# Four-layer graph network in one kernel: the third layer's rows in edge order, two PSUM banks per copy in every merge, and projected and normalised row as one 2 KB line per node

## What is computed

```python
h = jnp.maximum(_layernorm(x, axis=-1), 0.0)          # every layer begins so
...
proj_s = feature @ W_s.T                               # third layer, feature = h
proj_t = feature @ W_t.T
z = proj_s[src] + proj_t[dst]
z = jnp.where(z >= 0, z, NEG_SLOPE * z)
e = (z @ W_attn.T)[:, 0]
...                                                    # softmax of e over the edges of one source: alpha
msg = feature[src] * alpha[:, None]
agg = jax.ops.segment_sum(msg, dst, num_segments=n)
return agg @ W_fc.T + b_fc
```

## Time and profile before

| | us |
|---|---|
| median of 3 runs (lowest, highest) | 7961.38 (7960.68, 7969.36) |
| the profiled execution: its time | 7962.39 |
| the profiled execution: its span, first instruction to last | 7960.7 |
| node pass of the third layer | 847 |
| score pass | 1034 |
| merge 0 / 1 / 2 / 3 | 540 / 595 / 601 / 502 |

### The profile page before, as it was taken

The page is one execution under the profiler, slowest core; times in us unless marked ns, Lnnn a source line. Parts: engine busy times, 40 slices in busy tenths (PEclk is TensorE's granted clock), DMA queues, the critical chain, the costliest instruction groups (busy, mean ns, idle before and its releaser), DMA issues. The chain is left out here.

```text
span 7960.7 us, 152645 instructions
## 1 busy us (share of the span) xinstructions
PE 5847.9 (73%) x22090; PEld 3555.4 (45%) x22091; DVE 5333.9 (67%) x17864; ACT 3368.9 (42%) x10659; POOL 4364.3 (55%) x5571
## 2 busy tenths in 40 slices
PE   4997899847779997777999777777657679400477
PEld 3773244335534443554444344444225558400365
DVE  5999888745579994456666566666954569533755
ACT  1993255315645552454444333333113567300166
POOL 1556777700022224766777677776567653577443
PEclk8996699979999998999999989888888999755799
DMA  2664333459867775787989766665026877522177
GB/s 61 211 209 134 101 102 105 133 169 312 298 212 249 251 248 195 261 298 260 314 310 314 267 202 202 204 205 178 2 68 227 291 256 227 138 55 54 56 228 235
DMA packets 897753, 1560.81 MB, mean 196 GB/s; under 512 B 129481, under 2 KB 638654, under 8 KB 897575
## 3 DMA queue, kind: packets, MB, share of 16 engines
q1 hardware_dynamic: 572230, 858.57, 32.8%
q10 hardware_dynamic: 188000, 410.91, 14.9%
q0 software_dynamic: 137344, 289.63, 12.9%
HBM read 861.24 MB, written 697.48 MB: 196 GB/s over the span
## 5 line engine op out<-in xcount | busy, mean ns | idle before, releaser
L1431 PE MATMUL merge_banks<-merge_rows,merge_mask 128*128 x6264 | 1573.5, 406 | 631.9 <-SPq L1362 301.6
L1431 PEld LDWEIGHTS merge_banks<-merge_rows,merge_mask 128*128 128x128 f32 x6264 | 1220.3, 201 | 985.0 <-issue 814.0
L2133 PE MATMUL node_p_out<-w,node_h_t 128*128 128x259 f32 (+2 forms) x4704 | 1434.5, 427 | 9.3 <-ACT node_h_t L2172 7.9
L1413 DVE TENSOR_SCALAR merge_mask<-ramp,dst_at,soft_at_step 128x128 f32<-128x128 f32 x2349 | 839.2, 363 | 874.6 <-PE merge_banks L1431 735.6
L1495 ACT COPY merge_total<-merge_banks 128x256 f32<-128x256 f32 x1568 | 577.4, 369 | 1024.3 <-PE merge_banks L1431 866.6
L1575 POOL DMA_INDIRECT merge_rows<-h,merge_take_i x816 | 784.9, 962 | 317.9 <-issue 210.2
L2046 POOL TENSOR_TENSOR node_inv_std<-node_var,node_minus_half 128x4 f32<-128x4 f32 x392 | 433.5, 1106 | 886.0 <-DVE node_var L1981 567.9
L2133 PEld LDWEIGHTS node_p_out<-w,node_h_t 128*128 128x128 f32 x4704 | 744.4, 190 | 261.7 <-issue 207.0
L2111 PE MATMUL node_p_turn<-ident,node_xn 128*128 128x128 f32 x3136 | 620.7, 280 | 196.5 <-DVE node_xn L1938 96.1
L2133 PE MATMUL node_p_out<-w,node_kept_t 128*128 128x512 f32 x1568 | 741.7, 596 | 0.0
L2111 PEld LDWEIGHTS node_p_turn<-ident,node_xn 128*128 128x128 f32 x3136 | 403.2, 141 | 748.9 <-issue 463.0
(11 more groups left out here) (563 smaller groups left out, 11087.8 us busy)
## 6 DMA issues: line engine op xcount, KB each, us to landing
merge_held<-own ACTq DMA_DIRECT2D x196, 512.0 KB, 5.8
x<-merge_total ACTq DMA_DIRECT2D x196, 512.0 KB
node_x<-x SPq DMA_DIRECT2D x196, 512.0 KB, 6.0
node_x<-in_x SPq DMA_DIRECT2D x194, 512.0 KB
merge_rows<-h_by_edge SPq DMA_DIRECT2D x408, 128.0 KB
h<-node_rows_h SPq DMA_DIRECT2D x98, 516.0 KB, 4.2
h_by_edge<-rank_src_of_src SPq DMA_DIRECT2D x49, 1024.0 KB
merge_held<-h ACTq DMA_DIRECT2D x98, 512.0 KB, 5.7
```

What stands on the lines that cost most here:

```text
L1413: ins = nc.vector.tensor_scalar(mask[j][:], k.ramp[:, 0:P], columns(k.dst_at, s), columns(weight, s), ALU.is_equal, ALU.mult)
L1431: nc.tensor.matmul(banks[:, bass.ds(nc.s_assert_within(at[2 * j + 1], 0, (BANKS - 1) * 512, skip_runtime_bounds_check_because=small), D)], ...
L2133: ins = nc.tensor.matmul(p_out[w][g % banks][:, 0:n], turned_rows(q.h, g)[:, c * P:(c + 1) * P], matrix[:, c, :], start=c == 0, stop=c == 1)
```

## The change

It has four parts.

1. In every merge ACT copies two banks per instruction, for the flush as for the seed (`two_banks`): it waits for the last step of the second tile of the pair. `flush_at` keeps every second entry, so that a read of it brings 8 entries.
2. In every merge the first two groups of base rows are loaded and the banks seeded from them, and only then the other twelve loads are issued.
3. The third node pass writes the normalised row next to the projected one, in `out`, and stores both as one line of 2 KB per node (`pair2`). `kept_t` and its store are gone; the cut rows lie in four buffers `h_t` as in the other layers.
4. The score pass gathers those 2 KB lines. PE turns the normalised half of each gathered tile (two transposes), ACT cuts it at zero, PE multiplies by the third matrix, and the product is stored as `by_edge`, one row for each edge. So merge 2 loads its rows in order by SP, as merge 0 does, and POOL keeps only the release loop there. POOL's gathers wait for the turn as well as for the sum.

The core of the diff:

```diff
@@ merge
-                nc.scalar.copy(bank(q, g), held[q.held][:, g, :]).then_inc(seeded, 1)
+                nc.scalar.copy(two_banks(q, g), held[q.held][:, g:g + 2, :]).then_inc(seeded, 2)
...
-                    at[:] = counts(act, flush_at, H * G, min(4, TURN - q.w) * G)
+                    at[:] = counts(act, flush_at, H * (G // 2), min(4, TURN - q.w) * (G // 2))
...
-                for g in range(G):
-                    act.wait_ge(steps, at[q.w % 4 * G + g])
+                for g in range(0, G, 2):
+                    act.wait_ge(steps, at[(q.w % 4 * G + g) // 2])
...
-                    nc.scalar.copy(total[q.total][:, g, :], bank(q, g)).then_inc(kept, 1)
+                    nc.scalar.copy(total[q.total][:, g:g + 2, :], two_banks(q, g)).then_inc(kept, 2)
...
-            for n in range(HELD):
+            for n in range(2):
                 hold(At(0, n))
             act.wait_ge(opened, BANKS)
             for n in range(2):
-                for g in range(G):
+                for g in range(0, G, 2):
                     seed(At(0, n), g)
+            for n in range(2, HELD):
+                hold(At(0, n))
@@ node_pass
-    out = both("out", {0: [P, 1, G, D + 3], 1: [P, 1, G, D], 2: [P, 2, G, D], 3: [P, 1, G, P + 8]}[layer])
+    out = both("out", {0: [P, 1, G, D + 3], 1: [P, 1, G, D], 2: [P, G, 3, D], 3: [P, 1, G, P + 8]}[layer])
...
-                    parts = [out[q.h][:, n] for n in range(2)] + [biased[q.h][:]]
+                    parts = [out[q.h][:, :, 0:2, :].rearrange("p g n f -> p g (n f)"), out[q.h][:, :, 2, :], biased[q.h][:]]
...
-                if layer == 2:
-                    sp.dma_start(turned_group(tables[3], q.H), kept_t[q.h][:].rearrange("p g f -> p (g f)")
-                                 ).then_inc(t_put[q.h], 16)
@@ score_sources
-    a, b = ([ph.sb(f"{n}{j}", [P, D]) for j in range(R)] for n in "ab")
+    a, b = ([ph.sb(f"{n}{j}", [P, w]) for j in range(R)] for n, w in (("a", 2 * D), ("b", D)))
...
                         pool.wait_ge(added, t + LAG - R)
+                        pool.sem_inc(turn_pool, 1)
+                        pool.wait_ge(turned, t + LAG - R)
                         pool.sem_inc(turn_pool, 1)
...
+                    if j % LAG == 0:
+                        pe.wait_ge(got[j // LAG], 16 * 2 * LAG * (i + 1))
+                    turn(t, j, first)
                     if not (first and j < 2):
+                        multiply(t - 2, (j - 2) % R, first and j >= 2)
+                    if not (first and j < 3):
+                        place(t - 3, (j - 3) % R, first and j >= 3)
...
                         lower(t - 1, (j - 1) % R, first)
+                        rectify(t - 1, (j - 1) % R, first and j >= 1)
@@ gnn_kernel
-        merge(nc, k, "merge2", own2, x3, table=h2, weight=at_step)
+        merge(nc, k, "merge2", own2, x3, ordered=by_edge, weight=at_step)
```

More of the change, by code:

```diff
@@ L1472, in hold, with two_banks @@
                     act.dma_start(held[q.held][:], tile_rows(base, q.group() * ROWS)).then_inc(held_got[q.held], 16)
-            def bank(q, g):
+            def two_banks(q, g):
                 first = q.side * G + g
-                return banks[:, first * 512:first * 512 + D]
+                return banks[:, first * 512:(first + 2) * 512].rearrange("p (n f) -> p n f", n=2)[:, :, 0:D]
             def seed(q, g):
@@ L1770, in node_pass, with normal @@
     minus_half = ph.sb("minus_half", [P, G])
-    if layer == 2:
[L1772 to L1778, removed]
-    out = both("out", {0: [P, 1, G, D + 3], 1: [P, 1, G, D], 2: [P, 2, G, D], 3: [P, 1, G, P + 8]}[layer])
+    h_t = [ph.sb(f"h_t{n}", [P, D]) for n in range(G)]
+    out = both("out", {0: [P, 1, G, D + 3], 1: [P, 1, G, D], 2: [P, G, 3, D], 3: [P, 1, G, P + 8]}[layer])
     junk = [ph.sb(f"junk{n}", [P, D]) for n in range(2)]
+    def normal(side, g):
+        return out[side][:, g, 1, :] if layer == 2 else xn[side][:, g, :]
     p_turn = [ph.ps(f"p_turn{n}", [P, 512]) for n in range(2)]
@@ L2166, in rectify @@
                 act.wait_ge(turned, t + 1)
-                if layer == 2:
-                    if not q.new and g == 0:
-                        act.wait_ge(t_put[q.h], 16 * n_put * q.i)
-                elif not q.first:
+                if not q.first:
                     act.wait_ge(product, t - G + 1)
-                nc.scalar.activation(turned_rows(q.h, g), p_turn[g % 2][:, 0:D], ACT.Relu).then_inc(rectified, 1)
+                nc.scalar.activation(h_t[g][:], p_turn[g % 2][:, 0:D], ACT.Relu).then_inc(rectified, 1)
             def work(q):
@@ L2187, in work @@
                     if layer == 2:
-                        nc.scalar.copy(out[q.h][:, 0:2, g, :], p_out[0][g % banks][:].rearrange("p (n f) -> p n f", n=2)
+                        nc.scalar.copy(out[q.h][:, g, 0::2, :], p_out[0][g % banks][:].rearrange("p (n f) -> p n f", n=2)
                                        ).then_inc(out_made, 1)
@@ L2357, in _, with turn, multiply, place @@
         def _(pe):
+            def turn(t, j, first):
+                if not (first and j == 0):
+                    pe.wait_ge(rectified, t)
+                for c in range(2):
+                    ins = nc.tensor.transpose(p_turn[:, c * P:(c + 1) * P], a[j][:, D + c * P:D + (c + 1) * P], k.ident[:])
+                ins.then_inc(turned, 1)
+            def multiply(t, j, first):
+                pe.wait_ge(rectified, t + 1)
+                if not (first and j == 0):
+                    pe.wait_ge(h_made, t)
+                for c in range(2):
+                    ins = nc.tensor.matmul(p_h[:, 0:D], h_t[j % RING][:, c * P:(c + 1) * P], k.w2[:, c, 2 * D:3 * D],
+                                           start=c == 0, stop=c == 1)
+                ins.then_inc(product, 1)
+            def place(t, j, first):
+                pe.wait_ge(low_hot, t + 1)
+                pe.wait_ge(high_hot, t + 1)
+                nc.tensor.matmul(p_table[:, 0:NT], at_low[j % HOT][:], at_high[j % HOT][:], start=first and j == 0,
+                                 stop=False, skip_group_check=True).then_inc(placed, 1)
             def tiles(i, first, n):
@@ L2385, in keep_product @@
                 act.wait_ge(product, t + 1)
-                nc.scalar.copy(h[side][:, g, :], p_h[j % 2][:, 0:D]).then_inc(h_made, 1)
+                nc.scalar.copy(h[side][:, g, :], p_h[:, 0:D]).then_inc(h_made, 1)
             def lower(t, j, first):
@@ L2420, in _ @@
         def _(sp):
-            def load(q):
-                if not q.new:
-                    sp.wait_ge(product, G * q.last)
-                sp.dma_start(h_t[q.h][:].rearrange("p g f -> p (g f)"), turned_group(turned_in, q.H)).then_inc(h_got[q.h], 16)
             def store(q):
@@ L2430, in store @@
                 sp.dma_start(tile_rows(h_out, q.H * ROWS), h[q.h][:]).then_inc(h_put[q.h], 16)
-            pipeline(sp, groups, [(0, load), (3, store)], apart=2)
+            pipeline(sp, groups, [(0, store)])
             for side in range(S):
```

70 lines of the change are left out of this document (35 added, 35 removed).

## The result

The changed kernel takes 7846.57 us (median of 4 runs, 7830.40 to 7855.24) against 7965.37 for the kernel before, timed beside it: a ratio of 0.9848, 95% interval 0.9828 to 0.9867. That is 118.8 us less; 7814 was forecast, in a range of 7745 to 7912. The profiled execution took 7851.53 us, with a span of 7849.8, 110.9 under the span before.

| stage | before, us | after, us | measured | forecast |
|---|---|---|---|---|
| merge 0 | 539.7 | 515.0 | -24.7 | -25 |
| merge 1 | 595.1 | 584.0 | -11.1 | -8 |
| merge 2 | 600.9 | 534.0 | -66.9 | -85 |
| merge 3 | 502.1 | 489.7 | -12.4 | -33 |
| score pass | 1033.6 | 1028.0 | -5.6 | +8 |

The account below looks back on a forecast made before the run. Bounds differed by stage: POOL's gathers in the score pass, a near balance in the third node pass, gathers, DMA or ACT in the merges. -33 - 25 - 8 - 85 + 8 - 5 = -148 against 7962.39 gave 7814, range 7745 to 7912.

Parts of the forecast that it names:

- The far bounds of the merges: All four merges at the largest saving of their ranges: given as -215 us in sum, 7747 us in total.
- Merge 3, -33: Rest of merge 3: two-bank copies bring ACT from 409 to 348 us, under PE's 356; 370 taken, bounds 0 and -47.
- Merge 2, -85: Merge 2: loading rows in order gives -60 us, early banks -10, two-bank copies -15; bounds -50 to -105.
- Merge 0, -25: Merge 0: two-bank copies give -15 us where DMA bounds most of the rest, early banks give -10.
- Merge 1, -8: Merge 1: first chunk stays gather-bound, POOL's gathers and DMA stay close in the rest; -8 us, bounds 0 to -25.
- Early banks, -10 twice: Start of merges 0 and 2: banks seeded after two loads, 12 us earlier in merge 0; -10 us in each.
- Score pass, +8: Score pass: 2 KB gathers cost no more, POOL's added wait per block costs 8 us; 0 to +29.
- Third node pass, -5: Third node pass: work and bytes stay, one store less is issued; -5 us, bounds +10 to -64.
- The pair rival: Merges: PE waiting for seeds gives back all that two-bank copies save; -77 us, 7885; chance 0.17.
- The consumers: Score pass: becomes bound by its consumers, a tile taking 2.9 us instead of 2.63; 7912; chance 0.07.
- gather paid by bytes: Score pass: a 2 KB row costs POOL double; +372 us, 8186; chance 0.06.
- The joined line: Third node pass: the joined store ends DVE's 232.9 us wait, the pass runs at PE's 760 + 23; 7755; chance 0.1.

Follow-up runs that it names:

- the padded version: The changed kernel with 64 tiny ACT copies ahead of merge 2's loop, which move the loops of merges 2 and 3 by 4 KB: 7823.22 us.
- run 9: The changed kernel with the 64 tiny ACT copies, and PE waiting for masks and release once per four steps instead of twice per step: 7717.00 us.
- runs 1, 2 and 4: Changed kernel with ACT's merge loop written out, 7832.91 us; with 64 tiny ACT copies before merge 2's loop, 7823.22; with all base rows loaded before seeding, 7839.24.
- run 3: The changed kernel with ACT copying one bank per instruction again for flush and seed, the rest kept: 7904.17 us.
- run 5: The changed kernel with the 64 tiny ACT copies, and PE's read of 16 addresses per eight steps cut into two of 8: 8011.20 us.

## Why the prediction was right, and where it was not

The time came out inside the range and 32.6 us over the forecast. The stages' misses are larger than that: merges 2 and 3 gave 39 us less than forecast, and the misses of the score pass (14 us better) and of the third node pass (13 us worse) cancel by luck. The far bounds of the merges add up to -220, which with +8 and -5 is -217 and 7745, not -215 and 7747.

*Merge 3, -33 against -12.4: the step that failed is PE's pace.* The prediction took 4.39 us for eight steps from two neighbouring rows and made 356 us of it for the whole rest, far enough below ACT's sum for most of ACT's saving to come off. That is the pace with an address read near the shortest. With the mean of the changed kernel, (139.6/98 - 1.10) = 0.32 us more per eight steps, 649 steps take (4.39 + 0.32) x 649/8 = 382, and the padded version took 385. It could have been seen beforehand: in the kernel before, the 98 reads of merge 3 add up to 136.1 us, a mean of 1.39, which gives 380. ACT's terms were right within 5%: 409 us of ACT for the rest before, and with one bank and a fast PE it took 391; 348 with two banks, and it took 339 in run 9. (A read of `flush_at` fell from 1.79 to 1.20 us on the mean in merge 3, by 0.59 where 0.5 was taken.) So the gain stopped at PE, 21 us below the 403 of before, where PE's pace had been put 47 below. A second thing came on top: the branch gaps, which merge 3 had not had; they cost 2 to 7 us by runs 1, 2 and 4.

*Merge 2, -85 against -66.9.* The ordered rows did most of what was said: the first chunk went from 156 to 120 us (105 was expected, with the early banks' 10), and the stage to 534, 19 us above merge 0's 515, which has no gaps. The copies gave 17.3 where 15 was forecast. The early banks gave none of their 10. The gaps stayed, which no term had; in the padded version, without them, merge 2 takes 522.9, 78 less than before.

*Merge 0, -25 against -24.7, by the wrong sum and so by luck.* Its loop lost its 16.2 us of gaps, which no term had; the early banks' 10 didn't come, and its first chunk ends at 119 us instead of 115. "DMA bounds most of it" was half true: run 9 took a further 31.6 us out by PE's waits alone before the DMA engines were full. *Merge 1, -8 against -11.1*, lost 15.7 us of gaps in the same way; how much of its gain is the copies' was not parted.

*Early banks, -10 twice.* The seeds came even earlier than forecast, 17 us instead of 12, since the two loads were issued in 0.99 us and not 3. The step that failed is the next, that the start is worth anything while the rows queue up behind 6 MB of base rows on full DMA engines. The sentence on rows landing beside the twelve loads was there and was priced at 2 us.

*Score pass, +8 against -5.6.* The price of a gather was right, 964 ns against 968; the wait was covered. The blocks follow each other every 10.3 us as before; some 5 us went from the end of the stage, behind the last gather (17.2 us instead of 22.0), which no term had.

*Third node pass, -5 against +8.2.* On one chip the difference between joined and separate stores is nothing. The Trainium skill (DMA: Bandwidth & Descriptors, section Bandwidth) has the rule that a DMA should be batched to 1 MiB or more for 75% of the peak, measured there on loads issued from GpSimd. It doesn't show in these stores from SP: 1 MB in one DMA and in two of 512 KB take the same in a pass with 0.87 of DMA share.

*The rivals.* The pair rival named the right place, PE and ACT close to each other in merge 3, and the wrong mechanism: run 3 shows the pair gaining. The consumers never bound the score pass (POOL's idle time before its gathers is the same, 104.9 and 119.5 us). No gather paid by bytes. The joined line freed nothing: DVE still waits 241.3 us for the pass's stores, against 232.9.

## What to carry to other kernels

Two engines that are close in a stage are compared by their mean pace over the stage, waits for register reads and all, not by two neighbouring rows: the fastest rows of the engine off the path say how fast it can be once, not what it will give when the other gets out of the way. On an engine with many small instructions, count the waits: 12 of 16 taken out per eight steps were worth 106 us, nearly as much as the whole change. And look behind the branch of every long loop, in each copy of it, since the same loop left ACT idle for 5 us per turn in one place and not at all in another.

## What the runs showed of the hardware

- Behind a branch back in ACT's loop over two chunks ACT stood for 3.7 to 6.8 us in some copies of the loop and for 0.2 in others, with loads of 8 KB of instructions beside the long ones; 64 small instructions ahead of it took all of these gaps away, in two loops. The Trainium skill says of this (Runtime: NRT & Kernel Launch, section Instruction fetch mechanics) that a taken branch out of the instruction window has to wait for a DMA, and names blocks of 16 KiB; the gaps agree with the rule, the trace shows 8 KB pieces here.
- A read of 16 registers on PE takes 1.10 us at the least and up to 3.13 in the changed kernel, one of 8 takes 0.59 to 2.46 in run 5. Reads of other engines overlap 126 of the 167 that take over 1.2 us in the changed kernel, and 112 of the 225 shorter ones; that they are the cause was not tested.
- On PE's sequencer a step with its two waits took 0.34 us in the padded version, and 0.13 without a wait of its own in run 9.
- A copy of 512 columns by ACT takes 584 to 589 ns over two PSUM banks and 586 out of one.
- A gather of 128 rows by POOL costs the same for 4 B and 1 KB and for 2 KB rows: 963, 968 and 964 ns.
